# A transformer layer in float32: the first group's entry into the semilinear stage moved into the last group of the sampled attention

## The reference

```python
x = x + xattn(ctx, ctx, layernorm(x), mask, ...)      # sampled ("deformable") attention
x = x + attn(layernorm(x), ...)                       # semilinear attention with a recurrent state
x = x + ffn(layernorm(x), ...)                        # one of 8 experts for each token

# xattn: 16 heads of 32; each query reads 5 positions of K and V, linearly interpolated
Qp = q @ Wq.T + bq;  off = Qp @ Woff.T + boff         # where to sample
ix = positions from (query index + {-3..1} + off), modulo the length
scores = <Qp, 0.5*(w0*K[i0] + w1*K[i1])> / sqrt(32);  attn = softmax over the 5 samples
out = (sum attn * sampled V) @ Wo.T + bo

# attn: q, k, v = short_conv(h @ Wq), ... (4 causal taps and the input itself)
# lr = softplus(h @ Wlr + 0.001)
# two chunks of 16 tokens, in order; each updates W_in (4x32 per head) and W_out by softmax
# scores of the chunk and two inner steps of attention between the weights and the chunk
# out = o @ Wo
```

## Time and profile before

| | us |
|---|---|
| median of 3 runs (lowest, highest) | 1219.69 (1217.71, 1220.15) |
| the profiled execution, its own time | 1217.85 |
| its span | 1216.1 |
| projections, up to the first load of the sampled attention | 0 to 115.5 |
| sampled attention, up to the last store | 115.5 to 480.0 |
| semilinear stage, first DVE instruction | 483.5 |
| group(FIRST) of it begins on PE | 535.1 |
| experts begin | 1087.6 |

### The profile page before, as it was taken

The page is one execution under the profiler, slowest core; times in us unless marked ns, Lnnn a source line. Parts: engine busy times, 40 slices in busy tenths (PEclk is TensorE's granted clock), DMA queues, the critical chain, the costliest instruction groups (busy, mean ns, idle before and its releaser), DMA issues. The chain is left out here.

```text
span 1216.1 us, 18598 instructions
## 1 busy us (share of the span) xinstructions
PE 1061.4 (87%) x6220; PEld 787.6 (65%) x6220; DVE 813.3 (67%) x1592; ACT 494.7 (41%) x954; POOL 320.2 (26%) x265
## 2 busy tenths in 40 slices
PE   5993999999999963698999999999999987875997
PEld 4883566666666652477878776968696876763443
DVE  4565286778778883357888787979688876633332
ACT  1220255776676774134444443434252534310110
POOL 0344376677577662000000000000000000011553
PEclk9997898989889975788999999999899987765999
DMA  4281410222021000100010101010010031046541
GB/s 153 87 333 59 82 42 1 59 58 57 2 58 35 18 18 32 56 1 35 1 53 1 53 2 54 1 53 2 2 53 1 18 105 70 36 159 261 158 144 58
DMA packets 59924, 75.12 MB, mean 62 GB/s; under 512 B 37758, under 2 KB 42302, under 8 KB 57792
## 3 DMA queue, kind: packets, MB, share of 16 engines
q1 hardware_dynamic: 52384, 53.05, 13.7%
q0 software_dynamic: 5152, 12.59, 3.2%
q10 hardware_dynamic: 2304, 8.39, 1.7%
HBM read 56.71 MB, written 22.81 MB: 65 GB/s over the span
## 5 line engine op out<-in xcount | busy, mean ns | idle before, releaser
L1196 POOL COPY fw_x<-fw_x 128x1024 f32<-128x1024 f32 x8 | 8.3, 1040 | 536.0 <-DMA xh_scr<-fw_x 502.4
L556 POOL TENSOR_TENSOR aw_wtent<-aw_tent,aw_e 128x1760 f32<-128x1760 f32 x32 | 100.7, 3145 | 114.1 <-DVE aw_e L552 114.1
L745 PE MATMUL aw_psum_kv<-all_xWv,aw_c 128*128 128x512 f32 x256 | 124.6, 633 | 0.0
L528 POOL TENSOR_TENSOR aw_tent<-all_const,all_ix 128x1760 f32<-128x1760 f32 x32 | 100.6, 3145 | 5.1 <-POOL aw_wtent L556 4.6
L851 ACT ACTIVATE aw_cT<-aw_psum_av 32x256 f32<-32x256 f32 x128 | 80.5, 629 | 38.7 <-PE aw_psum_av L774 37.6
L733 PE MATMUL aw_psum_kv<-aw_c,all_xWk 128*128 128x352 f32 x256 | 81.6, 474 | 9.5 <-POOL aw_A L632 9.5
L2020 PE MATMUL ex_psum_y<-ex_We,ex_gT 128*128 x184 | 85.0, 607 | 0.0
L745 PEld LDWEIGHTS aw_psum_kv<-all_xWv,aw_c 128*128 128x128 f32 x256 | 49.4, 203 | 52.9 <-issue 51.1
L539 DVE TENSOR_TENSOR aw_prod<-aw_tent,aw_psum_s 128x1760 f32<-128x1760 f32 x32 | 63.5, 1984 | 23.8 <-ACT aw_tent L534 17.3
L1510 PE MATMUL fw_psum_front<-all_xWo,fw_cT 128*128 128x512 f32 x128 | 66.0, 666 | 11.7 <-DMA fw_cT<-c_scr 11.4
L733 PEld LDWEIGHTS aw_psum_kv<-aw_c,all_xWk 128*128 128x128 f32 x256 | 49.0, 196 | 35.2 <-POOL aw_A L632 9.6
(11 more groups left out here) (265 smaller groups left out, 2256.7 us busy)
## 6 DMA issues: line engine op xcount, KB each, us to landing
ex_We<-expert SPq DMA_DIRECT2D x1, 8192.0 KB, 22.4
aw_craw<-ctx SPq DMA_DIRECT2D x8, 704.0 KB, 4.8
xh_scr<-fw_x SPq DMA_DIRECT2D x10, 512.0 KB, 3.6
pj_x<-x_tok SPq DMA_DIRECT2D x8, 512.0 KB, 3.6
q_scr<-pj_QT ACTq DMA_DIRECT2D x8, 512.0 KB, 2.9
aw_Qb<-q_scr SPq DMA_DIRECT2D x32, 128.0 KB, 3.4
c_scr<-aw_cT ACTq DMA_DIRECT2D x8, 512.0 KB, 2.7
fw_cT<-c_scr SPq DMA_DIRECT2D x8, 512.0 KB, 4.8
```

The source lines that it names most:

```text
L528: return nc.gpsimd.tensor_tensor(self.tent[r][:], bc(rows, 1, self.nu * NK), bc(ix, 2, self.wr), ALU.subtract)
L556: return eng.tensor_tensor(self.wtent[:], self.tent[r][:], bc(self.e[:].rearrange("p u k -> p (u k)"), 2, self.wr), ALU.mult)
L745: mm = nc.tensor.matmul(ps_kv[:, j % 2, :], rows, Wv[:, c, :], start=(c == 0), stop=(c == KC - 1))
```

## The change

The entry of group 0 of the semilinear stage, from the projection `y0` to the spread rates, is issued in group 7 of the sampled attention. Its buffers are laid over buffers of the sampled attention: `Qblk[0]` becomes the common tile `wide` (4096 numbers a partition: `cT`, `x`, `x1`, `h`), the two context tiles `cw` become `even` and `odd` (`hT`, q, k, v), and the two PSUM banks `ps_kv`, used for keys and values, become a ring of two banks, `lead`, in place of the four of `front`. SP issues the four loads (groups 0 and 1) behind the last query load. `lead.prepare` (`wsum`) runs on DVE at the start of the sampled attention. 21 semaphores of the entry get their start value on POOL at the start of the sampled attention, and 17 of them were among the 46 of the semilinear stage before. POOL adds 4 counts there for the fills that `front` no longer makes. The general form of the attention runs the same entry in a block of its own (`lead_phase`), which these inputs do not reach.

```diff
+FRONT = [("y0", "dve"), ("y1", "dve"), ("t0", "act"), ("t1", "act"), ("q2", "dve"), ("q1", "dve"), ("v1", "dve"),
+         ("k2", "dve"), ("k0", "dve"), ("lr", "dve"), ("q0", "dve"), ("k1", "dve"), ("v0", "dve"), ("q3", "dve"),
+         ("k3", "dve"), ("v3", "dve"), ("v2", "dve"), ("ra", "dve")]
+CONV = [n for n, _ in FRONT if n[0] in "qkv"]
+LEAD = ([("y0", "dve"), ("y1", "dve"), ("t0", "act"), ("t1", "act"), ("lr", "dve")] + [(n, "dve") for n in CONV] + [("ra", "dve")])
+class Lead:
...
+        self.ring, self.opened = Ring(m, "lead", 2, LEAD, ps=False), 0
...
+    def load(self, sp):
+        sp.dma_start(self.cT, self.a["c_scr"][0]).then_inc(self.c_in.sem, 16)
+        sp.dma_start(self.xs, self.a["x_lb"][0].rearrange("p t d -> p t d")).then_inc(self.x_in.sem, 16)
+        sp.wait_ge(self.x1_done.sem, self.x1_done.at(0, 1))
+        sp.dma_start(self.cT, self.a["c_scr"][1]).then_inc(self.c_in.sem, 16)
+        sp.dma_start(self.xs, self.a["x_lb"][1]).then_inc(self.x_in.sem, 16)
...
 # attend_window_phase
-        cw = [m.sb(f"c{p}", [P, KC, BG, 64]) for p in two]
-        Qblk = [m.sb(f"Qb{p}", [P, KC, BG, P]) for p in two]
+        cw = [k[n][:].rearrange("p (c b m) -> p c b m", c=KC, b=BG) for n in ("even", "odd")]
+        Qblk = [k["wide"][:].rearrange("p (c b n) -> p c b n", c=KC, b=BG), m.sb("Qb1", [P, KC, BG, P])]
 # sync
+            sp.wait_ge(s_ps.sem, s_ps.at(NG - 2, PAIRS))
+            lead.load(sp)
 # gpsimd
             m.start(pool)
+            lead.start(pool)
 # vector, group(t, last)
                 scores(t, 2)
+                if last:
+                    lead.enter(dve)
                 weights(t, 1)
...
                 softmax(t, 2)
+                if last:
+                    lead.entered(dve)
                 scores(t, 3)
                 weights(t, 2)
                 softmax(t, 3)
...
+                if last:
+                    lead.rates_in(dve)
+                    lead.convolve(dve, *CONV[:2])
                 weights(t, 3)
+                if last:
+                    lead.rates_add(dve)
+                    lead.convolve(dve, *CONV[2:6])
+                    lead.rates_out(dve)
+                    lead.convolve(dve, *CONV[6:])
+                    lead.rates_spread(dve)
 # tensor, group(t, last)
                 scores(t, 3)
...
+                if last:
+                    pe.wait_ge(v_cp.sem, v_cp.at(t.r, PAIRS))
+                    lead.y(pe, 0)
+                    lead.y(pe, 1)
                 turn(t, 1)
                 context(t, 0)
...
                 turn(t, 2)
                 context(t, 1)
...
+                if last:
+                    lead.turned(pe)
+                    lead.rates(pe)
+                    lead.fill(pe, CONV[0])
                 context(t, 2)
+                if last:
+                    lead.fill(pe, CONV[1])
...
                 turn(t, 3)
+                if last:
+                    lead.fill(pe, CONV[2])
...
                 context(t, 3)
+                if last:
+                    for name in CONV[3:]:
+                        lead.fill(pe, name)
+                    lead.first(pe)
 # scalar, group(t, last)
                 context(t, 0)
                 turned(t, 1)
+                if last:
+                    lead.deviation(act)
                 weights(t, 3)
...
                 context(t, 1)
                 turned(t, 2)
...
+                if last:
+                    lead.copied(act)
                 context(t, 2)
+                if last:
+                    lead.base(act, *CONV[:2])
                 turned(t, 3)
+                if last:
+                    lead.base(act, CONV[2])
...
                 context(t, 3)
+                if last:
+                    lead.rates_exp(act)
+                    lead.base(act, *CONV[3:6])
+                    lead.rates_ln(act)
+                    lead.base(act, *CONV[6:])
 # fast_phase: vector, and likewise tensor and scalar
-            enter(FIRST)
-            entered(FIRST)
-            convolve(FIRST, CONV[:5])
-            rates_in(FIRST)
-            rates_add(FIRST)
-            convolve(FIRST, CONV[5:])
-            rates_out(FIRST)
-            rates_spread(FIRST)
             group(FIRST, False, False)
```

More of the change, by code:

```diff
@@ L196, with __init__ @@
 class Ring:
-    def __init__(self, m, name, banks, plan):
-        self.ps = m.ps(name, [P, banks, 512])
+    def __init__(self, m, name, banks, plan, ps=None):
+        self.ps = m.ps(name, [P, banks, 512]) if ps is None else ps
         self.names = [n for n, _ in plan]
@@ new lines, in lead_phase, with _ @@
+def lead_phase(nc, lead):
+    with ExitStack() as ctx:
+        lead.open(ctx)
+        block = ctx.enter_context(nc.Block())
+        @block.sync
+        def _(sp):
+            lead.load(sp)
+        @block.gpsimd
+        def _(pool):
+            lead.start(pool)
+        @block.vector
+        def _(dve):
+            lead.prepare(dve)
+            lead.enter(dve)
[7 more added lines that the diff above has]
+            lead.rates_spread(dve)
+        @block.tensor
+        def _(pe):
+            lead.y(pe, 0)
+            lead.y(pe, 1)
+            lead.turned(pe)
+            lead.rates(pe)
+            for name in CONV:
+                lead.fill(pe, name)
+            lead.first(pe)
+        @block.scalar
+        def _(act):
+            lead.deviation(act)
+            lead.copied(act)
+            lead.rates_exp(act)
+            lead.base(act, *CONV[:6])
+            lead.rates_ln(act)
+            lead.base(act, *CONV[6:])
@@ L581, in attend_window_phase @@
+def attend_window_phase(nc, a, k, lead):
     U = 2 * KC
@@ L1080, in fast_phase @@
         front, back = Ring(m, "front", 4, FRONT), Ring(m, "back", 4, BACK)
-        cT, xs = m.sb("cT", [P, KC, GT]), m.sb("x", [P, TT, D])
-        x1 = [m.sb(f"x1{p}", [P, TT, D]) for p in range(2)]
-        h, x2 = m.sb("h", [P, TT, D]), m.sb("x2", [P, TT, D])
+        cT, xs, h, hT = lead.cT, lead.xs, lead.h, lead.hT
+        x1 = [lead.x1, m.sb("x11", [P, TT, D])]
+        x2 = m.sb("x2", [P, TT, D])
         stats, mv, rstd = m.sb("st", [P, TT, 6]), m.sb("mv", [P, TT, 2]), m.sb("rs", [P, TT])
-        hT = m.sb("hT", [P, KC, GT])
-        f = [{n: m.sb(f"{n}T{p}", [P, KC, GT]) for n in "qkv"} for p in range(2)]
+        f = [lead.f, {n: m.sb(f"{n}T1", [P, KC, GT]) for n in "qkv"}]
         lr = m.sb("lr", [P, TT, 2 * H])
-        lrs = [m.sb(f"lrs{p}", [P, TT, 2 * H]) for p in range(2)]
-        lrf = [m.sb(f"lrf{p}", [P, KC, 2]) for p in range(2)]
+        lrs = [lead.lrs, m.sb("lrs1", [P, TT, 2 * H])]
+        lrf = [lead.lrf, m.sb("lrf1", [P, KC, 2])]
         chunks = range(L // C)
@@ L1105, in fast_phase @@
         bo, conv, wi, wt, wr = w["xbo"], w["conv"], w["aWin"], w["aWout"], w["aWout_rows"]
-        wsum = m.sb("wsum", [P, 3, KC])
+        wsum = lead.wsum
         const = k["const"]
@@ L1172, in _ @@
             sp.dma_start(Wg[:], a["gate"]).then_inc(wg_in.sem, 16)
-            load(FIRST)
-            load(FIRST.next())
             rounds(sp, NG, group, 1)
@@ L1189, in _ @@
             m.start(pool)
+            for c in (front.filled, conv_done, *front.read.values()):
+                pool.sem_inc(c.sem, c.per)
             def keep(t):
@@ L1216, in _ @@
             st.link(last)
-            st.link(nc.vector.tensor_scalar_add(wsum[:], conv[:, :, :, 3], 1.0))
             nc.vector.memset(top[:], 0.0).then_inc(setup.sem, 1)
@@ L1679, in group @@
                     gate_turn(3)
-            ahead(FIRST, *[x for x, _ in FRONT])
             pe.wait_ge(setup.sem, setup.at(0, 1))
@@ L1816, in group @@
                     gate_copy(2)
-            deviation(FIRST)
-            turned(FIRST)
-            base(FIRST, *CONV[:5])
-            rates_exp(FIRST)
-            base(FIRST, *CONV[5:])
-            rates_ln(FIRST)
             group(FIRST, False, False)
@@ L2042, in layer @@
         k["ones"] = k["const"][:, CONE:CONE + 1]
+        k["wide"] = m.sb("wide", [P, 4 * KC * GT])
+        k["even"], k["odd"] = (m.sb(n, [P, 2 * KC * GT]) for n in ("even", "odd"))
+        lead = Lead(nc, ctx, a, k)
         project_phase(nc, a, k)
```

175 lines of the change are left out of this document (158 added, 17 removed).

## The result

The change makes the kernel slower: 1230.7 us median of 7 runs against 1218.6 of before in the same session, ratio 1.0102, 95% interval [1.0068, 1.0136]. A second session, of four runs, gave 1233.4 and 1.0141 [1.0100, 1.0181]. The forecast was 1228.5, slower.

What follows compares the result with a forecast made beforehand. Bound: latency of two chains merged into one strict order per engine, each waiting for the other. +8.2 us up to the first semilinear group and +1.5 for counts make +9.7 on 1217.85; forecast 1228.5, own range 1223 to 1234, 8-in-10 range 1219.5 to 1237.

Steps and rivals of the forecast that it cites:

- The walk: Last attention group with the entry merged in, step by step from 450.4; the block was to end at 538.1.
- `aw_A` late: Last attention group: DVE's sums of pairs 1, 2 and 3 come 11, 19 and 38 us later than before.
- DVE idle 9 us before the residual's add: Sign in the last attention group: DVE stands idle some 9 us, waiting for PE.
- Fills at 2.0 us in the ring of two: End of the entry: with two banks, fills take 2.0 us each against 1.72 in the ring of four.
- The boundary: Between the sampled attention and the semilinear stage: costs 0.3 to 0.9 us, taken as 0.6.
- The set-up: Start of the semilinear stage: work hidden before beside the entry's loads and projections is bare, 4.4 to 4.6 us.
- The lead-in: Up to PE's start of the first semilinear group: at 543.3 instead of 535.10, +8.2 us.
- The counts, +1.5: Start of the sampled attention: 21 more counts on POOL delay PE's first keys by 1.5 us, on the path.
- PE is idle before it in both kernels, so the clock inside it is alike: First semilinear group: PE comes to it from idle before and after, so no clock difference was counted.
- The table load: ACT's load before the root in the entry: 1.28 us with no drain; by the skill page 1.4 later, sum +11.1.
- the clock stays up: Rival: the entry's matmuls keep PE at 2.4 GHz from 450 on, saving 13.2 us, 1214.4; chance 0.07.
- Hides it after all: Rival: the chains overlap and PE's idle time hides part of the entry, gain about 15 us, 1203; chance 0.03.

Runs made afterwards that it cites:

- e7_best: e6_setup with the semilinear stage's start counts moved into POOL's idle time and the entry's ring on four banks instead of two; 0.9878 of before.
- e6_setup: e2_woven with DVE's set-up of the semilinear stage moved into DVE's wait for the rates in the last attention group; 0.9951 of before.
- e11_pad: The changed kernel with 13 small matmuls of no use on PE at the start of the sampled attention; 1.0074 of before.
- e5_hot: The changed kernel with 13 matmuls of no use in PE's idle time before the first semilinear group; 1.0126 of before.
- e4_warm: The changed kernel with 30 matmuls of no use in PE's waits of the last attention group; 0.9988 of before.
- e2_woven: The changed kernel with the entry merged in another order, no step waiting ahead of attention work that is ready; 0.9952 of before.
- e9_warm_best: e7_best with 11 matmuls of no use, 5 and 6, in two of PE's waits of the last attention group; 0.9796 of before.

## Why the prediction was right, step by step

Offsets are from the end of PE's scores of pair 3, 450.4 in the forecast and 447.0 in the trace.

- **The walk.** Projections: +10.0 forecast, +8.5 measured (8.71 us instead of 9.99, more of them at the high level). `aw_A` of pair 1: +16.2 / +14.6; `h`: +25.2 / +23.7; `aw_A` of pair 2: +31.9 / +30.2; `hT`: +39.7 / +37.6; `aw_A` of pair 3: +57.1 / +53.7; end of the block: +87.7 / +84.7. Every wait is where the walk put it. It is 3 us too long: 1.5 in the projections, 0.4 in the copies to `hT`, 0.9 in context 2, which took 1.16 us as the clock had risen; the small rest is spread.
- **`aw_A` late** by 11, 19 and 38 us: measured 6.4, 14.0 and 31.3 in clock times, to which the 3.35 us of the early start belong: 9.7, 17.3 and 34.6.
- **DVE idle 9 us before the residual's add:** 3.72 and 2.67, 6.4 us. DVE's scores of pair 2, which end at 448.5, took the beginning.
- **Fills at 2.0 us in the ring of two:** 2.04 in the mean of the last seven (514.80 to 529.07); the one ahead of them met the low clock (3.67). The step was right, and e7_best shows what the ring costs.
- **The boundary** 0.6: 1.0. **The set-up** 4.6: 5.25. Of that, 0.83 is one copy of DVE that took 0.99 us beside POOL's copy. The lead-in came out at +6.2 and, the second time, +7.9 to +8.1, against +8.2 forecast. What the step missed is that the set-up was not the last thing there: by e6_setup, taking it away gives nothing, since PE's first four transposes end as late (8.0 us behind the spread, against 7.8).
- **The counts, +1.5:** 1.64 measured at POOL's first memset, and 1.3 to 1.7 still there 65 us on. At the first store it is not seen, where traces of one code differ by 4 us. So the size is right, and that it is paid in the end is not shown.
- **"PE is idle before it in both kernels, so the clock inside it is alike":** nearly. PE was at 1.00 until 532 and idle for 2.5 us up to 534.9; after, it stands idle for 8.2. The first 8 us were at 0.57 and 0.59 in the traces of before and at 0.50, 0.50 and 0.53 (e11_pad) with the change, the next 16 at 0.89 and 0.93 against 0.91, 0.93 and 0.91. The first group took 95.4, 93.7 and 92.7 (e11_pad) against 92.1, 92.7 and 92.7: 1.4 us in the mean, with a scatter of the same size. e5_hot suggests, by one trace, that coming to it at 2.4 GHz is worth 3 to 6 us there; both kernels begin it near 0.5.
- **What nobody had priced** is the loop, 4 to 7 us over before, by waits marked issue in steps that were not changed and by a lower clock in the same stretches. With the waits gone (e11_pad) the ratio is 1.0074, 9 us, and its interval, 5 to 13 us, holds the forecast's +9.7. There the trace has +6.1 in the lead-in and 0.0 to 0.6 in the first group.
- **Where luck helped.** The mechanism, two chains that wait for each other, is shown, and its +8.2 came out as +6.2 to +8.1. That the whole is so near is partly luck. In the two profiled executions of the first session (+10.9, of which the stretches named here make 10.7) the lead-in is +6.2, the first group +3.3 and the loop +4.4, and the sampled attention ahead of the change -3.3 by scatter; the forecast had +1.5 for the counts in place of the last three. The runs lie 2.2 us (1230.7) and 4.9 us (1233.4) above the forecast, about the size of what the loop adds.
- **The table load:** ACT's root stands at 469.26, directly behind the load (467.97, 1.28). The trace again shows no drain, against the 1.38 us of the Trainium skill, "ScalarE: Activation LUTs", section "What ACT_TABLE_LOAD costs".
- **Of the rivals,** "the clock stays up" has a price that is not confirmed. It was put at 13.2 us (its own terms, with three turns and four contexts halved, give 13.9), and e4_warm, which keeps the clock at 0.96 up to 480 with idle instructions, has a lead-in 8.0 us shorter than after and 9.6 than its second trace. Of the 13.2, 3.1 were for the projections, which took 8.33 us there and 8.71 in after. Its condition did not occur: the granted clock was 0.50 to 0.51 from 460 to 490. "Hides it after all" is true of another order: e2_woven, and e9_warm_best at 2.0%.

## What to carry to other kernels

Two latency chains that are merged into one strict order per engine fill each other's gaps only if each step is placed behind the other chain's work that is ready sooner; walk both with the durations of the trace, and ask of each wait what stands queued behind it. Where PE had waited, the steps behind came at the lower clock: filling the waits gave 8.0 us (e4_warm) and 6.0 (e9_warm_best), the better order 18.8. Before a difference under 1% is put down to a change, look for waits marked issue in untouched loops, and shift the code by a few idle instructions as a control: thirteen moved the unchanged kernel by 0.88%.
